# First cross attention: the inverse roots of the query and key norms as one power instruction on GpSimd in place of Newton steps on VectorE

## The reference

```
def _rmsnorm(t):
    return t * rsqrt(mean(t * t, axis=-1) + 1e-06)
q = x @ Wq.T;  k_raw = context @ Wk.T;  v_raw = context @ Wv.T   # 32 heads of 16
q = _rmsnorm(q);  k = _rmsnorm(k)
scores = einsum('bhnd,bhmd->bhnm', q, k) * HEAD_DIM ** -0.5
out = einsum('bhnm,bhmd->bhnd', softmax(scores), v)
```

## Time and profile before

| | |
|---|---|
| median of 3 runs | 1530.09 us (1528.89 to 1531.1) |
| the profiled execution, its own time | 1531.7 us |
| its span, first to last instruction | 1529.9 us |
| mean granted TensorE clock over the span | 0.953 |
| this stage in the profile | about 12 to 450 us |
| PE busy over the span | 1413.6 us (92%) |
| DVE, ACT, POOL busy | 999.5, 783.1, 78.4 us |

### The profile page before, as it was taken

How to read it: one execution, slowest core, us unless ns; L and a number is a source line. 1 busy time by engine, 2 the same in 40 slices (tenths; PEclk the granted TensorE clock), 3 DMA queues, 4 the chain that set the end, 5 groups by cost and what they waited for, 6 DMA issues and landing times. The chain is left out here.

```text
span 1529.9 us, 31878 instructions
## 1 busy us (share of the span) xinstructions
PE 1413.6 (92%) x11766; PEld 1088.1 (71%) x11772; DVE 999.5 (65%) x1651; ACT 783.1 (51%) x1130; POOL 78.4 (5%) x71
## 2 busy tenths in 40 slices
PE   4899999999969889999989999968999688899998
PEld 2677776777735468999977787745666365799997
DVE  6566677666644557766646877867999343576664
ACT  2677777777740635555422222227888103455552
POOL 0000000000001400000001111120000000000000
PEclk8999999999989989999999999988999768899999
DMA  4333443433333058566205233227885120576662
GB/s 152 76 83 82 110 110 84 83 87 87 63 84 132 1 195 264 189 209 209 79 28 179 97 122 111 83 74 172 174 174 126 48 53 1 189 258 216 216 216 76
DMA packets 133312, 190.93 MB, mean 125 GB/s; under 512 B 74955, under 2 KB 96685, under 8 KB 130030
## 3 DMA queue, kind: packets, MB, share of 16 engines
q1 hardware_dynamic: 133247, 190.04, 42.8%
HBM read 153.86 MB, written 17.48 MB: 112 GB/s over the span
## 5 line engine op out<-in xcount | busy, mean ns | idle before, releaser
L185 PE MATMUL psum<-m_x_hi,m_gu_hi 128*128 128x256 f32 x780 | 222.9, 286 | 1.1 <-DVE m_h L2366 0.9
L186 PE MATMUL psum<-m_x_hi,m_gu_lo 128*128 128x256 f32 x780 | 222.2, 285 | 0.0
L187 PE MATMUL psum<-m_x_lo,m_gu_hi 128*128 128x256 f32 x780 | 222.0, 285 | 0.0
L1512 DVE TENSOR_REDUCE x_peaks<-psum 128x2048 f32 (+1 forms) x64 | 146.3, 2291 | 51.6 <-PE psum L1404 51.6
L185 PE MATMUL psum<-x_w_hi,x_ctx_hi 128*128 128x256 f32 x512 | 158.8, 310 | 11.7 <-DVE x_ctx_lo L531 11.7
L185 PEld LDWEIGHTS psum<-m_x_hi,m_gu_hi 128*128 128x128 f32 x780 | 150.7, 193 | 4.8 <-issue 1.9
L186 PEld LDWEIGHTS psum<-m_x_hi,m_gu_lo 128*128 128x128 f32 x780 | 150.8, 193 | 1.5
L187 PEld LDWEIGHTS psum<-m_x_lo,m_gu_hi 128*128 128x128 f32 x780 | 150.6, 193 | 0.0
L186 PE MATMUL psum<-x_w_hi,x_ctx_lo 128*128 128x256 f32 x512 | 144.8, 283 | 0.0
L187 PE MATMUL psum<-x_w_lo,x_ctx_hi 128*128 128x256 f32 x512 | 144.6, 282 | 0.0
L1642 DVE TENSOR_TENSOR e_wqp<-e_wqp,x_probs 128x1024 f32<-128x1024 f32 x124 | 141.7, 1219 | 3.0 <-ACT x_probs L1657 3.0
(11 more groups left out here) (310 smaller groups left out, 2775.0 us busy)
## 6 DMA issues: line engine op xcount, KB each, us to landing
m_gu_raw<-in_m_gu SPq DMA_DIRECT2D x41, 768.0 KB, 4.2
e_w<-x_keys_dram SPq DMA_DIRECT2D x45, 512.0 KB, 6.8
m_gu_raw<-in_m_gu SPq DMA_DIRECT2D x18, 1024.0 KB, 4.8
x_ctx_raw<-in_ctxT SPq DMA_DIRECT2D x64, 256.0 KB, 2.7
m_dn_raw<-in_m_down SPq DMA_DIRECT2D x16, 768.0 KB, 4.3
m_dn_raw<-in_m_down SPq DMA_DIRECT2D x18, 512.0 KB, 5.3
x_keys_dram<-x_keys_hi SPq DMA_DIRECT2D x16, 512.0 KB, 3.2
x_keys_dram<-e_wqp SPq DMA_DIRECT2D x16, 512.0 KB, 2.6
```

The costliest lines, as they stand in the source:

```text
L185: pe.matmul(out, a[0], b[0], start=start, stop=False, skip_group_check=True)
L186: pe.matmul(out, a[1], b[0], start=False, stop=False, skip_group_check=True)
L187: return pe.matmul(out, a[0], b[1], start=False, stop=stop, skip_group_check=True)
L1512: dve.tensor_reduce(peaks[:, t, 4 * m:4 * m + 4, bass.ds(k, 1)].rearrange("p h k -> p (h k)"), g.psum[:, at:at + BANKS, :], AX, ALU.max).t ...
```

## The change

The ten VectorE instructions of `rsqrt` go, and with them the function and its two temporary arrays. In their place POOL gets a program for this stage: one power instruction of 128x64 for the queries, and one of 128x32 for every pair of context tiles (32 in all). DVE waits for each before it goes on with the scaling. ACT's wait on `k_step` keeps its meaning (the squares have been summed) with new counts.

```diff
-def rsqrt(dve, y, x, t, done, count):
-    dve.tensor_scalar(y.bitcast(I32), x.bitcast(I32), -0.5, 1597463007.0, ALU.mult, ALU.add).then_inc(done, 1)
-    for i in range(3):
-        dve.wait_ge(done, count + 3 * i + 1)
-        dve.tensor_tensor(t, y, y, ALU.mult).then_inc(done, 1)
-        dve.wait_ge(done, count + 3 * i + 2)
-        dve.scalar_tensor_tensor(out=t, in0=t, scalar=-0.5, in1=x, op0=ALU.mult, op1=ALU.mult).then_inc(done, 1)
-        dve.wait_ge(done, count + 3 * i + 3)
-        dve.scalar_tensor_tensor(out=y, in0=t, scalar=1.5, in1=y, op0=ALU.add, op1=ALU.mult).then_inc(done, 1)
-    dve.wait_ge(done, count + RSQRT_STEPS)
...
@@ the program of GpSimd in this stage
+                def root_two(n):
+                    pool.wait_ge(k_step, 2 * n + 2)
+                    if not (isinstance(n, int) and n < 2):
+                        pool.wait_ge(k_scaled, 3 * n)
+                    pool.tensor_tensor(rs[:, :], ms[:, :], g.neg_half[:, 0:2 * HH], ALU.pow).then_inc(k_step, 2)
+
                 pool.memset(vals[:, :, :, XHD:XHD + 1], 1.0).then_inc(consts_ready, 1)
+                pool.wait_ge(q_step, NT + 1)
+                pool.tensor_tensor(q_rs[:, :], q_ss[:, :], g.neg_half[:, 0:NT * XH], ALU.pow).then_inc(q_step, 1)
+                root_two(0)
+
+                def body(n, s, at):
+                    if s % 2 == 0 and at + 3 < STEPS:
+                        root_two(n + 2)
+
+                turns(pool, body)
@@ ScalarE, before the squares of the keys
-                            act.wait_ge(k_step, 6 * n + 7)
+                            act.wait_ge(k_step, 2 * n + 3)
@@ VectorE, norm_two
-                    count = n * (K_STEPS // 2)
+                    count = n * 2
...
                     dve.wait_ge(k_step, count + 2)
-                    rsqrt(dve, rs[:, :], ms[:, :], rs_tmp[:, :], k_step, count + 2)
+                    dve.wait_ge(k_step, count + K_STEPS)
@@ VectorE, the queries
                 dve.wait_ge(q_step, NT + 1)
-                rsqrt(dve, q_rs[:, :], q_ss[:, :], q_tmp[:, :], q_step, NT + 1)
-                count = NT + 1 + RSQRT_STEPS
+                dve.wait_ge(q_step, NT + 2)
+                count = NT + 2
```

More of the change, by code:

```diff
@@ L187, in product3 @@
     return pe.matmul(out, a[0], b[1], start=False, stop=stop, skip_group_check=True)
-RSQRT_STEPS = 10
-def rsqrt(dve, y, x, t, done, count):
-    dve.tensor_scalar(y.bitcast(I32), x.bitcast(I32), -0.5, 1597463007.0, ALU.mult, ALU.add).then_inc(done, 1)
-    for i in range(3):
-        dve.wait_ge(done, count + 3 * i + 1)
-        dve.tensor_tensor(t, y, y, ALU.mult).then_inc(done, 1)
-        dve.wait_ge(done, count + 3 * i + 2)
-        dve.scalar_tensor_tensor(out=t, in0=t, scalar=-0.5, in1=x, op0=ALU.mult, op1=ALU.mult).then_inc(done, 1)
-        dve.wait_ge(done, count + 3 * i + 3)
-        dve.scalar_tensor_tensor(out=y, in0=t, scalar=1.5, in1=y, op0=ALU.add, op1=ALU.mult).then_inc(done, 1)
-    dve.wait_ge(done, count + RSQRT_STEPS)
 def heads_of(a, d):
@@ L236, in stage_cross0 @@
         SLOTS = 4
-        K_STEPS = RSQRT_STEPS + 2
+        K_STEPS = 4
         q_rows = sb("q_rows", [P, XP, L], F16)
@@ L267, in stage_cross0 @@
         q_rs = sb("q_rs", [P, NT * XH], F32)
-        q_tmp = sb("q_tmp", [P, NT * XH], F32)
         qn = sb("qn", [P, NT, D], F32)
@@ L276, in stage_cross0 @@
         rs = sb("rs", [P, 2 * HH], F32)
-        rs_tmp = sb("rs_tmp", [P, 2 * HH], F32)
         k_raw = sb("k_raw", [P, SLOTS, HW], F32)
```

## The result

The changed kernel takes 1612.32 us (median of 4 runs, 1611.06 to 1616.38), the kernel before 1529.86 us (4 runs): a ratio of 1.054, with a 95% interval of 1.052 to 1.056, or +82.5 us. The forecast was slower with 72%, by 7.5 us; the range of 1526 to 1691 holds the time, but the size is off by a factor of eleven. What happened is the rival in which the loop is bound by the ring through the keys. The prediction gave it 24% and 16% in its two parts, together 40%, more than the 32% of the band that its number stands in.

What follows compares the result with a forecast made beforehand. VectorE's chain was taken to bound the prologue and PE the loop. Query norm +4.05, two key norms +1.33 each, the switch +0.80 and 29 hidden norms 0 gave +7.5 us, 1537.6 (about 1538) us; 8-in-10 range 1526 to 1691.

Steps and rivals of the forecast that it cites:

- the rival in which the loop is bound by the ring through the keys: Loop: late transposed keys delay every pair from 0.107 us a column; 1691 us at 0.25 (24% up to there, 16% above).
- the band that its number stands in: Whole kernel: 0.066 to 0.107 us a further column, slower by the prologue alone, 1533 to 1540 us; chance 32%.
- What bounds the kernel: Prologue set by VectorE's chain, with PE idle 11.73 us; loop bound by PE, busy 376.48 of 380 us.
- the faster case: Whole kernel: if power columns stream at 2.3 ns each, the prologue gains 4.9 us at most, 1525.2 us; chance 12%.
- What goes: VectorE's inverse-root steps: 2.47 us per 32-column key norm on the path, 2.80 us for the queries' 64 columns.
- The unknown price: POOL's power: 0.55 us for one column, each further one between 2.3 ns and 0.45 us, taken as 0.095 us.
- P32: Time of POOL's power instruction of 32 columns for a key norm, taken as 3.50 us.
- the other 29 of the 32 norms: 0, hidden by the 1.68 us: Loop: 29 key norms cost nothing, since transposed keys land 1.68 us before PE reads them; 0.35 us left.
- the switch: Switch between the halves: slack only 0.53 us, so the key norm there costs 1.33 - 0.53 = +0.80 us.
- What hides it in the loop: Loop: slack of 1.68 us in transposed keys; a ring of 8.52 us plus the 32-column power against PE's 12.37 us pair.
- the threshold: Loop: a 32-column power of up to 3.85 us keeps PE's pace; beyond it every pair gets longer.
- The sum: Query norm +4.05, first key norm +1.33, step 0 +1.33, change of halves +0.80, other norms 0: total +7.5 us.

Runs made afterwards that it cites:

- the queries-only kernel: The changed kernel with the POOL power for the queries alone, the keys keeping their Newton steps on VectorE: 1539.76 us, ratio 1.0054.
- the product kernel: The changed kernel with a product in place of both powers, inverse roots left out: 1522.2 us, ratio 0.9947 to the kernel before.
- the one by tile: The changed kernel with the keys' power in two instructions of 16 columns, each tile's scaling waiting for its own: 1543.18 us, ratio 1.0093.
- the kernel by tile with the splits moved: The changed kernel with 16-column key powers, context tile 2's split before the query norm and the other half's weight split before step 0: 1534.48 us, ratio 1.0024.
- the splits-first kernel: The kernel before, Newton steps kept, with context tile 2's split before the query norm and the other half's weight split before step 0: 1523.66 and 1520.06 us.

## Why the prediction was wrong

- *What bounds the kernel* was right. The prologue is VectorE's chain: the queries-only kernel pays 8.7 us for a norm that is 8.15 us longer, and moving splits out of the chain gives 7.4 and 11.7 us in its two measurements. The loop is PE's: the product kernel and the one by tile keep its pace. The cap of 4.9 us on the faster case was too low: the product kernel gained 8.9, and the clock behind a shorter wait, the likely cause of the difference, stood in no term.
- *What goes* was right: 2.47 and 2.80 us were what the profile gave back.
- *The unknown price* is the step that failed. I took 0.095 us for a further column; it is 0.160. So P32 was 5.43 us and not 3.50, and the term "the other 29 of the 32 norms: 0, hidden by the 1.68 us" broke with it: the gaps between the powers of the loop, the switch among them, became 61.7 us longer. The bounds (0.0023 and 0.45) held it. The argument for a fifth of the high end, that later columns share most of the first one's fill, has nothing in the runs behind it: the first column costs the same 0.16 us over a fixed part of 0.39. My high end charged that fixed part to the column, since I took the launch from a memset (0.10 us).
- *What hides it in the loop*: the mechanism, a ring against PE's pace, was right. The ring was taken 0.4 us too short: by the prediction's own formula it is 8.52 + 5.43 = 13.95 at 5.43 us; measured 14.35. With that the threshold is 12.37 - (14.35 - 5.43) = 3.45 us and not 3.85, and my choice of 3.50 had no room left. No run has a power between 2.90 and 5.43 us on the ring, so the threshold is worked out and not measured. Of the 0.4, 0.15 us is the way to POOL (225.28 - 224.87 = 0.41, where I had 0.26 with the longer small instruction counted in), 0.08 the way back (230.83 - 230.71 against 0.04), and the rest small differences in the DMA's issue and landing.
- *The sum* with the measured price would have been 8.1 for the queries, 6.5 for two key norms, 2.7 at the switch and 29 x 1.58 = 46 in the loop: 63 us, against 82.5. The switch paid what the formula says (16.75 us in the changed kernel, and 360.4 less 28 x 12.37, which is 14.0, before). What the sum lacks is the 0.4 us of the longer ring in 28 pairs (11 us), the long pairs with their lower clock (3.6 us, which are 422.1 less 16.75 and 28 x 14.35), 0.9 us behind the last norm (2.5 in place of 1.6), 0.3 us in the query norm and the first two key norms, and the 0.95 and 2.4 us that lie ahead of the change or outside the stage. The lower clock in the loop stood beside the ring-bound rival, without a price.
- *The chances.* The ring-bound case had 40% in its two parts (24% up to 0.25 us a column, where the measured 0.160 lies), my own band 32%: by these chances the number of the forecast stood in a case less likely than the one beyond the threshold. The margin between my choice and the threshold was 0.35 us in 3.50, while the price was open by a factor of 190: with so steep a cost beyond the threshold, a forecast just below it was the wrong place to stand.

The Trainium skill's GPSIMD Engine Reference, section 3.1, with 2.6 cycles a column for two inputs, would have made this a gain. It holds roughly for the product (2392 ns for 1024 columns, 2.8 cycles each), and the product kernel is indeed 8.9 us faster; for the power it is off by a factor of 70. The rule of its section 7, that a dependent fp32 chain costs 4 cycles a step, points the right way: 0.160 us are 192 of the 1.2 GHz cycles that the page gives, so 48 such steps one after the other would make the time. That is an estimate from the page; no run here shows the inside of the instruction.

## What to carry to other kernels

An instruction whose cost is known for one column only has two numbers in it, a fixed part and a price per column, and they must be measured apart before it is widened; one short run with idle work of several widths did that here. Then ask on which ring the instruction lies and how much slack that ring has: about the same GpSimd work (5.43 and 5.8 us a pair) cost 62 us in the loop when the ring was 14.35 us long, and nothing that shows when it was 11.8, under the 12.37 of PE. On GpSimd the power is cheap for one column and dear for 32, where ten dependent VectorE instructions take 2.2 us. What gain there was with the roots computed came from neither way of taking the root, but from reading which instructions stood behind it in VectorE's queue without need.

## What the runs showed of the hardware

- A power on GpSimd (tensor by tensor, fp32) costs 0.39 us and 0.160 us for each column of 128 rows, the same for the base 1.0 as for real data. A product of 32 columns costs 0.25 us.
- A wait of some 2 us in every pair of steps left TensorE's granted clock at 1.00 in most pairs and took it down to 0.50 for a few us in about every fourth, in the pair read here (148.74 us) 1.4 us after the engine had resumed; waits of 7 us in every pair brought a long window's mean to 0.81, with 0.50 from the first work behind the wait on (211.99 to 216.33 us). The lower clock adds to a ring where the work done at it is on the ring.
- Two powers of 16 columns take 6.33 us beside VectorE's scaling of the queries, and 5.77 us (one row, 39.76 us, of the kernel by tile with the splits moved) with VectorE at its wait. The Trainium skill's page SBUF — State Buffer, in its section "Who interferes with whom", says that a VectorE instruction with two SBUF inputs contends with a GpSimd one that reads SBUF. The rows agree with it: the first power started beside a VectorE instruction with one input from PSUM and took 6.33 - 3.45 = 2.88 us, as alone; the second started at 30.38 us, within two VectorE instructions with two SBUF inputs (29.78 to 31.07 us), and took 3.45. These two VectorE instructions were not held up (1.29 us, as in the splits-first kernel), so here it was GpSimd that gave way. That such a power is held only at its start fits the 10.54 us of the 64 columns too, but no experiment was made for it.
